# A graph network's head: transfers, slot rows, one-hots and gather waits put in another order

## The reference, cut to what matters

```
x = layernorm(x + GAT2(relu(GAT1(x))))
x = layernorm(x + relu-MLP(x, segment_max(x[src] @ Ws + x[dst] @ Wd + w_e * ww + bm)))
# one attention layer:
h = (x @ W) ; e = leaky(a_src[src] + a_dst[dst]) ; ex = exp(e - segmax(e)[dst])
out = segment_sum(h[src] * ex / (segment_sum(ex)[dst] + 1e-16)) + bias
```

## Time and profile before

| what | value |
|---|---|
| median of 3 runs | 6849.09 us (6848.08 to 6849.81) |
| span of the profiled execution | 6856.8 us |
| its own time beside the span | none is given apart from the span |
| PE, ACT, DVE, POOL busy | 74%, 68%, 60%, 72% of the span |
| mean DMA rate | 138 GB/s |

### The profile page before, as it was taken

How to read it: one execution, slowest core, us unless ns; L and a number is a source line. 1 busy time by engine, 2 the same in 40 slices (tenths; PEclk the granted TensorE clock), 3 DMA queues, 4 the chain that set the end, 5 groups by cost and what they waited for, 6 DMA issues and landing times.

```text
span 6856.8 us, 136148 instructions
## 1 busy us (share of the span) xinstructions
PE 5089.9 (74%) x24591; PEld 4780.1 (70%) x24591; DVE 4096.0 (60%) x11895; ACT 4663.9 (68%) x10649; POOL 4951.3 (72%) x5220
## 2 busy tenths in 40 slices
PE   7988888888887798888888888764555556556556
PEld 6987888888786797887888788654455445445455
DVE  3655555555556465555555555565666666666667
ACT  5877777777776687777777777774555555555558
POOL 5777777777774777777777777557777777777772
PEclk6555555555555655555555555567888788888879
DMA  8444444444443554444444444365655665565564
GB/s 232 128 119 117 115 122 119 116 119 120 118 114 72 152 130 115 117 121 119 114 121 119 117 117 121 82 185 151 177 166 163 177 172 164 168 178 167 162 183 137
DMA packets 820595, 943.49 MB, mean 138 GB/s; under 512 B 185720, under 2 KB 549570, under 8 KB 819522
## 3 DMA queue, kind: packets, MB, share of 16 engines
q1 hardware_dynamic: 658962, 595.34, 30.1%
q0 software_dynamic: 160256, 335.36, 21.4%
q10 hardware_dynamic: 432, 2.45, 0.1%
HBM read 883.19 MB, written 49.44 MB: 136 GB/s over the span
## 4 chain that ended last, share of the span: by engine, by line
PE 36%; POOL 22%; issue 14%; DVE 12%; DMA 11%; DVEq 2%; ACT 2%; SPq 1%; POOLq 0%; ACTq 0%
POOL G L682 22%; PE bA L780 13%; PE bS L815 12%; DVE acc L1415 4%; DMA G<-table,idx 4%; PE bM L815 3%; PE bE L815 3%; DMA st<-d_neg 3%; DVE bA L1644 2%; DMA G<-ztable,idx 2%; DVE ch L1650 1%; PE bA L703 1%; DVE G L1482 1%; PE bP L703 1%; DVEq L1281 1%
## 5 line engine op out<-in xcount | busy, mean ns | idle before, releaser
L682 POOL DMA_INDIRECT G<-table,idx x3328 | 3148.2, 946 | 1051.1 <-issue 921.8
L815 PE MATMUL bS<-G,S 128*128 x8816 | 2036.6, 391 | 362.2 <-DVE acc L1415 211.5
L815 PEld LDWEIGHTS bS<-G,S 128*128 128x128 f32 x8816 | 1753.4, 280 | 479.5 <-issue 471.4
L682 POOL DMA_INDIRECT G<-ztable,idx x1664 | 1573.8, 946 | 524.1 <-issue 467.5
L1068 ACT ACTIVATE S<-iota_row,nd 128x128 f32<-128x128 f32 x5904 | 1864.2, 387 | 69.1 <-issue 40.7
L780 PEld LDWEIGHTS bA<-adst,st 128*128 128x128 f32 x7872 | 1797.2, 333 | 126.2 <-issue 122.4
L780 PE MATMUL bA<-adst,st 128*128 x7872 | 1698.0, 340 | 91.2 <-issue 71.0
L1415 DVE TENSOR_TENSOR acc<-acc,bS 128x136 f32 (+1 forms) x4408 | 1277.0, 290 | 580.7 <-DVE acc L1415 94.6
L1072 ACT ACTIVATE S<-S,one_col 128x512 f32<-128x512 f32 x1476 | 1065.2, 722 | 56.5 <-issue 7.0
L1054 ACT ACTIVATE st<-xr,neg_p 128x512 f32<-128x512 f32 x984 | 699.8, 711 | 531.3 <-DMA xr<-d_drel 331.2
L703 PE MATMUL bA<-ident,G 128*128 128x128 f32 x1664 | 328.4, 339 | 704.6 <-DVE ch L1650 582.2
(11 more groups left out here) (217 smaller groups left out, 3988.3 us busy)
## 6 DMA issues: line engine op xcount, KB each, us to landing
xr<-d_drel SPq DMA_DIRECT2D x984, 256.0 KB
xr<-in_ew SPq DMA_DIRECT2D x312, 256.0 KB
st<-d_neg SPq DMA_DIRECT2D x312, 256.0 KB
G<-table,idx POOLq DMA_INDIRECT x3328
G<-ztable,idx POOLq DMA_INDIRECT x1664
isend<-in_ew SPq DMA_DIRECT2D x104, 256.0 KB
isend<-d_neg SPq DMA_DIRECT2D x104, 256.0 KB
table<-G SPq DMA_DIRECT2D x48, 264.0 KB, 4.9
```

The lines of the kernel that those rows point to most:

```text
L682: pool.indirect_dma_start(G[:, r, c, 0:width], None, from_table, bass.IndirectOffsetOnAxis(ap=idx[:, r, c:c + 1], axis=0)).then_inc(gather ...
L815: mm = pe.matmul(bank_of(l, u, r, k)[:, j * w:(j + 1) * w], S[:, onehots(r, i), s, :], Gf[:, bass.ds(chunk_at[0][s], w)], start=True, stop ...
```

## The change

The first features are loaded ahead of the destination rows. `c_rest` and `ends_i` are no longer loaded by ScalarE's queue at the start but by SP after the seventh broadcast, and `ends_i` lies in another part of `acc`. The stores of `d_neg` and `d_goes` move behind the third slot store. TensorE transposes one block of slot rows after every fourth quad of the first 32 expanded, VectorE copies it out and SP stores it there, each store ahead of the broadcasts for quads 4n+7 to 4n+10. In the first layer every third quad of the first 36 gets its one-hot from VectorE, in one instruction. `isend` is made after all that. The weights of the second layer are prepared during the expansions. The waits of `pace` are gone; those on `sel_done` stay.

```diff
@@ -34,6 +34,7 @@
+FIRST_Q = 4 * UQ
@@ -216,9 +217,9 @@
-        ends_i = room(0, 2 * NCH).bitcast(I32).rearrange("p (a c) -> p a c", a=2)
+        ends_i = room(5024, 2 * NCH).bitcast(I32).rearrange("p (a c) -> p a c", a=2)
@@ -296,6 +298,14 @@
+        def hits_on_dve(q):
+
+            return q < FIRST_Q and q % 3 == 2
+        def act_quads(q):
+
+            return q - FIRST_Q // 3 if q >= FIRST_Q else q - q // 3
@@ -369,35 +379,36 @@
...
                 sp.dma_start(idx[:, r, :], d_idx[b]).then_inc(idx_in[r], 16)
 
             sp.dma_start(last_i, dst_last.rearrange("(a n) -> a n", a=1).to_broadcast([P, NCH])).then_inc(in_last, 16)
-            for g in range(4):
+            for g in range(XR):
                 x_load(g)
             sp.dma_start(rows_i, dst_rows.rearrange("(k q) f -> q k f", q=P)).then_inc(in_rows, 16)
-            for g in range(4, XR):
-                x_load(g)
             for r in range(RING):
                 idx_load(0, r, r, 0)
             for g in range(NG):
                 if g + XR < NG:
                     x_load(g + XR)
                 table_store(0, table[0], g)
-                if g == 16:
-                    sp.wait_ge(neg_made, 1)
-                    sp.dma_start(d_neg.rearrange("(k q) f -> q k f", q=P), neg).then_inc(neg_out, 16)
             sp.wait_ge(drel_made, 1)
             sp.dma_start(d_drel.rearrange("(j p) f -> p j f", p=P), drel).then_inc(drel_out, 16)
-            sp.wait_ge(tp_used, 1)
-            goes_to = d_goes.rearrange("(k n) a c -> a k n c", n=P // CB)
-            for a in range(2):
-                sp.dma_start(goes_to[a], goes_s[a * KQ:a * KQ + KB]).then_inc(goes_out, 16)
             sp.wait_ge(tp_used, 2)
             sp.dma_start(d_tbl.rearrange("k (j f) -> (k j) f", f=P), tbl_i).then_inc(tbl_out, 16)
 
-            def slot_stores():
-                for n in range(8):
-                    sp.wait_ge(tp_used, 2 + n + 1)
-                    sp.dma_start(d_nd[n // 4, :, n % 4 * 512:n % 4 * 512 + 512], Sf[n % 3]).then_inc(nd_out[n % 3], 16)
-                for n in range(3):
-                    sp.wait_ge(nd_out[n], 48 if n < 2 else 32)
+            def mask_stores():
+                sp.wait_ge(neg_made, 1)
+                sp.dma_start(d_neg.rearrange("(k q) f -> q k f", q=P), neg).then_inc(neg_out, 16)
+                sp.wait_ge(tp_used, 1)
+                goes_to = d_goes.rearrange("(k n) a c -> a k n c", n=P // CB)
+                for a in range(2):
+                    sp.dma_start(goes_to[a], goes_s[a * KQ:a * KQ + KB]).then_inc(goes_out, 16)
+
+            def late_inputs():
+                sp.dma_start(c_rest[:, :], rest).then_inc(in_rest, 16)
+                sp.wait_ge(cj_made, 1)
+                sp.dma_start(ends_i, dst_ends).then_inc(in_ends, 16)
+
+            def slot_store(n):
+                sp.wait_ge(tp_used, 2 + n + 1)
+                sp.dma_start(d_nd[n // 4, :, n % 4 * 512:n % 4 * 512 + 512], Sf[n % 3]).then_inc(nd_out[n % 3], 16)
 
             def mask_load(l, b, r, it):
                 free = l * NB + b - 1
@@ -429,34 +440,59 @@
...
                 for i in range(first, min(last, quads_of(u))):
-                    free = quad(l, u, i) - 2
-                    if due(free):
-                        sp.wait_ge(st_abs, free)
+                    q = quad(l, u, i) - 3
+                    if isinstance(q, int) and hits_on_dve(q) and due(q):
+                        sp.wait_ge(st_dve, q // 3 + 1)
+                        sp.nop(nofuse=True)
+                    elif not isinstance(q, int):
+                        sp.wait_ge(st_abs, q + 1 - FIRST_Q // 3)
+                        sp.nop(nofuse=True)
+                    elif q >= 0:
+                        sp.wait_ge(st_abs, act_quads(q) + 1)
                         sp.nop(nofuse=True)
                     rows = d_drel.rearrange("(q s) f -> q (s f)", s=QS)[bass.ds(u * UQ + i, 1)]
                     sp.dma_start(xrf[i % 3], rows.to_broadcast([P, QS * P])).then_inc(xr_in[i % 3], 16)
 
+            def first_loads():
+                sp.wait_ge(drel_out, 16)
+                sp.wait_ge(tbl_out, 16)
+                exp_load(0, 0, 0, 0)
+                drel_load(0, 0, 0, 3)
+                exp_load(0, 1, 1, 0)
+                drel_load(0, 0, 3, 7)
+                late_inputs()
+                for n in range(8):
+                    slot_store(n)
+                    for q in range(4 * n + 7, min(4 * n + 11, FIRST_Q)):
+                        drel_load(0, q // UQ, q % UQ, q % UQ + 1)
+                    if n % 2 == 1 and n < 7:
+                        exp_load(0, n // 2 + 2, n // 2 + 2, 0)
+                    if n == 2:
+                        mask_stores()
+                for n in range(3):
+                    sp.wait_ge(nd_out[n], 48 if n < 2 else 32)
+                sp.wait_ge(neg_out, 16)
+                sp.wait_ge(goes_out, 32)
+                for u in range(2):
+                    mask_load(0, u, u, 0)
+                    sel_load(0, u, u, 0)
...
@@ -660,7 +696,6 @@
 
-                            if l < 2 and pace[4 * b + m]:
-                                pool.wait_ge(ex_done, quad(l, 0, pace[4 * b + m]))
-                            elif b >= 2 and UQ * (b - 2) + 2 * m > lag:
+                            if b >= 2 and UQ * (b - 2) + 2 * m > lag:
                                 pool.wait_ge(sel_done, 2 * quad(l, b - 2, 2 * m - lag))
@@ -744,14 +777,21 @@
-            def setup_slots():
+            def setup_table():
                 pe.wait_ge(drel_made, 1)
                 turn(to_setup(1)[0:4 * JB, 0:P], jsm[:, 9:13, :].rearrange("p k j -> p (k j)")).then_inc(tp, 1)
-                for n in range(8):
-                    to, frm = to_setup(2 + n), (drel, nd_rows)[n // 4]
-                    for j in range(4):
-                        tr = turn(to[:, j * P:(j + 1) * P], frm[:, n % 4 * 4 + j, :])
-                    tr.then_inc(tp, 1)
+
+            def setup_slots(n):
+                to, frm = to_setup(2 + n), (drel, nd_rows)[n // 4]
+                for j in range(4):
+                    tr = turn(to[:, j * P:(j + 1) * P], frm[:, n % 4 * 4 + j, :])
+                tr.then_inc(tp, 1)
+
+            def setup_weights():
+                pe.wait_ge(in_rest, 16)
+                pe.matmul(bM[:, 0:2 * HEADS], WT[1], att[1], start=True, stop=True)
+                pe.matmul(bM[:, P:2 * P], WdT, U1a, start=True, stop=True)
+                pe.matmul(bM[:, 2 * P:2 * P + 1], U1a, bmc, start=True, stop=True).then_inc(attw, 1)
@@ -759,15 +799,11 @@
             for g in range(NG):
                 multiply_group(0, g)
                 if g == 3:
-                    pe.wait_ge(in_rest, 16)
-                    pe.matmul(bM[:, 0:2 * HEADS], WT[1], att[1], start=True, stop=True)
-                    pe.matmul(bM[:, P:2 * P], WdT, U1a, start=True, stop=True)
-                    pe.matmul(bM[:, 2 * P:2 * P + 1], U1a, bmc, start=True, stop=True).then_inc(attw, 1)
                     pe.wait_ge(consts, 8)
                     pe.wait_ge(pads, 1)
                 if g == 18:
                     setup_goes()
-            setup_slots()
+            setup_table()
@@ -775,7 +811,13 @@
-                pe.wait_ge(st_made, quad(l, u, i) + 1)
+                q = quad(l, u, i)
+                if not isinstance(q, int):
+                    pe.wait_ge(st_made, q + 1 - FIRST_Q // 3)
+                elif hits_on_dve(q):
+                    pe.wait_ge(st_dve, q // 3 + 1)
+                else:
+                    pe.wait_ge(st_made, act_quads(q) + 1)
@@ -821,9 +863,12 @@
-                for u in range(4):
-                    for i in range(UQ):
-                        expand_quad(l, u, u, 0, i)
+                for q in range(FIRST_Q):
+                    expand_quad(l, q // UQ, q // UQ, 0, q % UQ)
+                    if l == 0 and q % 4 == 3 and q < FIRST_Q - 4:
+                        setup_slots(q // 4)
+                    if l == 0 and q == 3 * UQ - 1:
+                        setup_weights()
@@ -1012,8 +1057,6 @@
             act.dma_start(c_first[:, :], first).then_inc(in_first, 16)
-            act.dma_start(c_rest[:, :], rest).then_inc(in_rest, 16)
-            act.dma_start(ends_i, dst_ends).then_inc(in_ends, 16)
@@ -1054,8 +1097,15 @@
             def hits(l, u, r, it, i):
-                act.wait_ge(st_abs, quad(l, u, i) + 1)
+                q = quad(l, u, i)
+                act.wait_ge(st_abs, act_quads(q) + 1 if isinstance(q, int) else q + 1 - FIRST_Q // 3)
+
+            def second_weights():
+                act.wait_ge(attw, 2)
+                attention(1, bM)
+                act.activation(WdU[:, :], bM[:, P:2 * P], ACT.Copy)
+                act.activation(bmu, bM[:, 2 * P:2 * P + 1], ACT.Copy).then_inc(attw_used, 1)
@@ -1080,10 +1130,12 @@
-                for u in range(4):
-                    for i in range(UQ):
-                        distance(l, u, u, 0, i)
-                        hits(l, u, u, 0, i)
```

(66 more changed lines are left out.)

## The result

The changed kernel takes **6868.08 us** (median of 8 runs, 6866.16 to 6869.53), against 6849.41 for the kernel before (8 runs, 6848.08 to 6851.17): ratio 1.0026, interval [1.0017, 1.0035], **18.7 us slower**. By the bound of 0.2% named in the prediction that is a small loss. The profiled execution took 6868.55 us, with a span of 6866.7. The profiled span of the kernel before, 6856.8, is itself 7.4 us longer than that kernel's median time, so the two spans differ by only 9.9.

What follows compares the result with a forecast made beforehand. GpSimd's gathers bound the first layer, and the head's first logits decide when they run on. First logits at 172.3 put gather 161 10.1 us later: 6849.1 + 10.1 = 6859 us, range 6844 to 6871.

Steps and rivals of the forecast that it cites:

- slower by more: Rival on store, broadcast and one-hot: broadcasts land in 4.5 us, first logits at 186.3, 6873 us; chance 0.26.
- Gathers' start: GpSimd's first gather at about 60.6 us; gather 161 could start at most 18.1 us earlier without pace.
- First expansion: TensorE starts expanding at 71.4 us instead of 86.98; the first four quads end at 78.3.
- One-hot on VectorE: VectorE's one-hot costs between nothing and 0.69 us; TensorE waits 1.8 us at quads 8, 20 and 32.
- The rings: Seven stretches between ends of quads 4n+3 and 4n+7 take 64.6 us, 9.1 or 9.6 each, before late loads.
- late inputs: c_rest and ends_i in SP's queue before block 0 and quad 7 add 3.4 us; d_neg before block 3 adds 2.0.
- VectorE's tail: Behind quad 35's one-hot, isend and the clearing take 17.5 us before the first logits at 172.3, 15 us bare.
- Gather 161 at the first `logits` + 116.6: Batch 5's first gather needs quads 0 to 27 selected, done 116.6 us after the first logits, at 288.9.
- the 6.1 us of slack before: In the kernel before, quad 27 is selected at 272.7, 6.1 us before GpSimd uses it for gather 161.
- Feed keeps up: Rival: broadcasts land sooner and only TensorE counts; first logits at 160.8, 6848 us; chance 0.18.
- GpSimd bounds: Rival: VectorE's tail does not hold the first batch, the gathers give all 18.1 us, 6831 us; chance 0.07.
- does not do what it says: Rival: row gathers still bound the head, expansions start at 75, effects cancel within 0.2%; chance 0.05.

Runs made afterwards that it cites:

- e7: The changed kernel once more, unedited: 6862.9 us, ratio 1.0025 to the kernel before at 6844.78.
- e8: The kernel before with one wait added, so VectorE's clearing stands behind the last head expansion: 6855.51 us, ratio 1.0013.
- e9: The changed kernel with VectorE's clearing in pieces between its one-hots and each group's first broadcast ahead of the slot store: 6848.55 us, ratio 1.0004.
- e11: The kernel of e10 with c_rest and dst_ends issued from ScalarE's queue behind quad 3: 8624.54 us, ratio 1.0141.
- e2: The kernel before with only the pace waits taken away: 8714.23 us, ratio 1.0120 to the kernel before at 8611.99.
- e6: The changed kernel with pace waits back, VectorE's clearing in pieces and each group's first broadcast ahead of the store: 8517.41 us, ratio 1.0025.
- e12: The kernel before without the pace waits, as in e2, on another chip: 8615.28 us, ratio 1.0139.
- e1: The changed kernel with VectorE's tail (isend, es, clearing of acc) in pieces ahead of and between its one-hots: 8736.66 us, ratio 1.0128.
- e3: The changed kernel with the first broadcast of each group issued ahead of the slot store: 8721.06 us, ratio 1.0114.
- e10: The kernel of e9 with the first three broadcasts of unit 4 issued ahead of the masks: 8619.38 us, ratio 1.0143.
- e4: The changed kernel with the pace table and its wait put back: 8617.28 us, ratio 1.0004.

## Why the prediction was right, and which term was mis-sized

The forecast was 6859 us, 10.1 more than before, within the bound of no change by a little; the runs gave 18.7 more, inside the range (6844 to 6871). The way there was right, the size half of it. By the prediction's own division the result does not belong to the forecast: from 13.8 us, or a first `logits` at 176, it counted as the rival "slower by more", which had 0.26. The range, wide enough to take in most of that rival, holds it.

- **Gathers' start** 60.6, bound of 18.1 us: came at 58.49. Right that it is a bound; GpSimd waits at gathers 89 and 161 as named.
- **First expansion** 71.4, quad 3 at 78.3: 72.55 and 79.5. Right within 1.2.
- **One-hot on VectorE**, taken between nothing and 0.69: 0.48 or 0.49 in most, 0.69 at the longest; the waits of TensorE for it at quads 8, 20 and 32 are 1.27 to 1.43, predicted 1.8.
- **The rings**, 70.0 us with late inputs and `d_neg`: 78.8 (79.5 to 158.3). **This term was mis-sized**, and in it the price of a broadcast from issue to one-hot: 2.72, taken as 3.2 behind a store. Three rings that end on a one-hot of ScalarE show 5.7, 5.3 and 4.4 in its place. The other two, behind the late inputs and `d_neg`, show 9.1 and 7.05 where the forecast had 6.6 and 5.2. Each of the five is 0.9 to 2.2 us longer than forecast. The two that end on VectorE were forecast at 9.6 from TensorE's own work and took 9.5 and 9.6. The 2.72 was a wrong pairing: the broadcast issued at 116.89 is not the one that ScalarE's one-hot at 119.61 uses. SP's timeline of the kernel before has one just ahead of it,

```profile
115.53 0.33 SPq L437 DMA_DIRECT2D xr<-d_drel  x1
```

and from there to 119.61 are 4.1 us. Three buffers rotate, so an issue must be paired with the use by buffer, not by nearness. Two others that ScalarE stood waiting for took 3.15 (104.98 to 108.13) and 4.45 (110.28 to 114.73) in that trace. With 4.1 to 4.5 in place of 3.2 the same sum gives 0.9 to 1.3 more for each of the five rings and for the one-hot of quad 35, 5.4 to 7.8 in all. Missing were 10.6 at the first `logits` (182.94 against 172.3): 1.2 from the start, 8.8 in the rings, 0.5 at quad 35 and 0.1 behind it. By this estimate the wrong pairing is the larger part. Why a broadcast took up to 5.7 us in the changed kernel is not shown; in e7, the same kernel again, the rings took 75.2. The rival "slower by more" had named this place and 4.5 us; its other terms were too large (inputs 7, `d_neg` 4), for they cost about what the forecast had (3.4 and 2.0): among the rings that end on ScalarE, the first, with the inputs, is 14.7 us and the one with `d_neg` 12.7, against 11.3, 11.0 and 10.0 for the rest.
- **VectorE's tail**, 17.5 us from when the one-hot of quad 35 is ready: 17.6 (165.37 to 182.94). Right. e8 shows its largest part by itself: there the late clearing alone costs the kernel before 10.7 us.
- **Gather 161 at the first `logits` + 116.6**: 116.9, and 117.0 in e7 and e8. Right. Of the 26.8 us at the first `logits`, the 6.1 us of slack before leave 20.7, and 21.1 came. The time rose by 18.7 only; the 2.4 between stay unexplained.
- **Feed keeps up, GpSimd bounds, does not do what it says**: each is excluded by the rows of the result.
- **Not priced at all**: what `pace` protects from. "In the second layer `pace` costs nothing now" and its removal "could" only gain; on two other chips removing it from the kernel before costs 1.2 and 1.4%. Where that kernel takes 6845 to 6849 us no run puts `pace` back or takes it out by itself, so what share of the 18.7 us it has, or of the slow broadcasts, is open. e9, without it, is level with the kernel before, which bounds what is left over but does not give its price.

The order of descriptors in one ring (the Trainium skill, DMA: Bandwidth & Descriptors, Queues, rings and completion order) had been weighed for the late inputs. In the changed kernel quad 7's broadcast, issued at 81.69 behind them, was used at 90.78, 9.1 us later against 4.4 to 5.7 behind a store alone. The trace agrees with their going first, but the load of 2.3 MB on the same DMA engines would also delay it, and no run here tells the two apart (the 2.2 us of e11 come from a chip under contention).

## What to carry over

Work moved from an idle engine into the critical loop takes its cover away from everything behind it in that engine's list: after moving one-hots to VectorE, look first at what stood quietly beside the loop (here 15 us of clearing) and cut it into pieces. A first gather 12 us earlier is worth nothing while the consumer that frees its buffers is late; find the one landmark that the end follows at a constant distance (here first `logits` + 117 us, and only on the chips where the kernel takes 6845 to 6849) and price each edit by how it moves that. A wait that costs nothing in one trace may be what keeps two kinds of transfers apart; take it out only with a measurement on several chips.

## What the runs showed of the hardware

- Gathers issued back to back every 1.25 us from GpSimd (528 bytes a row, 54 GB/s) can stop transfers of the hardware queue almost wholly: one broadcast of 256 KB in about 21 us instead of some 4, with the DMA engines 0.28 busy (e2). It was so in all six traces without `pace` on two chips on which the kernel before takes 8496 and 8612 us, and in none of the three without `pace` (the changed kernel, e7, e9) where it takes 6845 to 6849. On a third chip of the first kind (8500) only kernels with `pace` ran; e6 waits 14.1 us for one quad there.
- The hold does not end with the gathers: the next one-hot starts 11.8 to 13.7 us after the last gather ended, in all six. Within it the DMA engines stand still: 0.01 busy in e2 (184 to 194 us), 0.00 in e12 (181 to 190) and in e1, e3 and e10 over 10 us.
- Pauses of 2.2 to 5.4 us ahead of every eighth gather were enough to keep the broadcasts coming (e4, 8617 us, ratio 1.0004).
- The kernel before takes 24 to 26% longer on some chips than on others; the granted clock over the span is 0.58 to 0.59 of full speed there and 0.62 on the others, which is 6% of it.
- A memset of 13328 fp32 columns on VectorE takes 11.16 us, 0.84 ns a column; the comparison `add, is_equal` over 128 x 512 fp32 from SBUF 0.49 us.
